# Filler products between the projections ahead of the first scores, and a new order of the third attention's slots, in a two-layer cross-attention transformer kernel

## What is computed

```python
# x: (16, 256, 128), ctx: (16, 64, 64), 16 heads everywhere
x = x + attn0(LN(x), ctx)     # causal self attention (8 channels a head) plus cross attention on ctx, one projection
x = x + ffn0(LN(x))           # silu(x w1) * (x w2) -> gelu(. h1) -> gelu(. h2) -> . w3, hidden 512, ternary weights
u = LN(LN(x)) * g + b         # then, inside the second layer's block:
u = u + mha(u, u)             # self attention, 32 channels a head, masked after the softmax, then a gelu FFN of 512
u = LN(u) * g2 + b2
x = x + u + mha(u, ctx)       # cross attention on 64 context rows, then a gelu FFN of 512
x = x + moe(LN(x))            # top-1 routing over 8 experts with 640 places each, hidden 512
```

## Time and profile before

| what | value |
|---|---|
| median of 3 runs | 1377.05 us (1377.03 to 1378.21) |
| the profiled execution's own time | 1379.22 us |
| its span | 1377.5 us |
| PE busy | 1270.9 us, 92% of the span |
| DVE, ACT, POOL busy | 973.8, 850.3, 656.3 us |
| mean granted TensorE clock | 0.975 of full speed |

### The profile page before, as it was taken

How to read it: one execution, slowest core, us unless ns; L and a number is a source line. 1 busy time by engine, 2 the same in 40 slices (tenths; PEclk the granted TensorE clock), 3 DMA queues, 4 the chain that set the end, 5 groups by cost and what they waited for, 6 DMA issues and landing times.

```text
span 1377.5 us, 43219 instructions
## 1 busy us (share of the span) xinstructions
PE 1270.9 (92%) x18030; PEld 826.5 (60%) x18030; DVE 973.8 (71%) x2245; ACT 850.3 (62%) x1333; POOL 656.3 (48%) x1129
## 2 busy tenths in 40 slices
PE   7999999997999999899999999989978888899895
PEld 4455555554455554456777777766755666676584
DVE  6788888875555554577888888766568887687343
ACT  3687777776666665657777777755456666542352
POOL 4456665633000002236667676544536776355265
PEclk6999999998999999999999999999999999999998
DMA  7000000000600000000011011012001111122451
GB/s 231 6 3 4 3 3 3 4 3 2 172 5 1 1 1 1 1 1 18 19 34 33 19 33 33 19 36 75 1 15 50 49 48 48 48 88 89 150 170 42
DMA packets 64097, 53.80 MB, mean 39 GB/s; under 512 B 10023, under 2 KB 58155, under 8 KB 63648
## 3 DMA queue, kind: packets, MB, share of 16 engines
q1 hardware_dynamic: 60000, 44.21, 11.0%
q0 software_dynamic: 2816, 6.11, 1.3%
q10 hardware_dynamic: 1088, 0.72, 0.2%
HBM read 20.35 MB, written 14.49 MB: 25 GB/s over the span
## 4 chain that ended last, share of the span: by engine, by line
PE 75%; DVE 13%; ACT 4%; issue 3%; POOL 3%; DMA 1%; SPq 0%; POOLq 0%; DVEq 0%; ACTq 0%
PE psum L1575 7%; PE psum L1603 4%; DVE a_nm L623 4%; PE psum L1236 4%; PE psum L960 4%; PE psum L962 4%; PE psum L961 4%; PE psum L1198 3%; PE psum L2696 3%; PE psum L381 2%; PE psum L1546 2%; PE psum L2051 2%; PE psum L535 2%; PE psum L1587 2%; PE psum L2671 1%
## 5 line engine op out<-in xcount | busy, mean ns | idle before, releaser
L1658 DVE TENSOR_REDUCE b_nm<-psum 128x4 f16<-128x1024 f32 x128 | 156.6, 1223 | 52.3 <-PE psum L1580 51.6
L740 ACT ACTIVATE a_prob<-psum 128x768 f32<-128x768 f32 (+1 forms) x160 | 136.1, 853 | 50.3 <-PE psum L467 48.6
L623 DVE TENSOR_REDUCE a_nm<-psum 128x4 f16<-128x1024 f32 (+1 forms) x96 | 117.2, 1222 | 26.2 <-PE psum L480 24.9
L792 POOL TENSOR_SCALAR_AFFINE_SELECT a_prob<-a_prob 128x512 f32<-128x512 f32 x128 | 84.4, 660 | 106.2 <-ACT a_prob L740 106.0
L171 POOL TENSOR_TENSOR f_ln_rstd<-f_ln_tmp,pow_half 128x4 f32<-128x4 f32 x24 | 24.4, 1018 | 194.0 <-DVE f_ln_tmp L160 193.9
L1088 ACT ACTIVATE xo_sb<-psum,f_w_h_s 128x512 f32<-128x512 f32 x64 | 44.0, 688 | 88.3 <-PE psum L962 88.3
L1575 PE MATMUL psum<-b_QTh,b_KTh 32*128 32x256 f16 x512 | 70.4, 272 | 7.3 <-DVE b_nm L1658 5.2
L1580 PE MATMUL psum<-b_KTh,b_QTh 32*128 32x256 f16 x512 | 70.7, 273 | 1.2 <-DVE b_nm L1658 1.2
L1580 PE MATMUL psum<-b_KTl,b_QTh 32*128 32x256 f16 x512 | 69.3, 268 | 0.0
L1580 PE MATMUL psum<-b_KTh,b_QTl 32*128 32x256 f16 x512 | 69.3, 268 | 0.0
L1575 PE MATMUL psum<-b_QTh,b_KTl 32*128 32x256 f16 x512 | 69.3, 268 | 0.0
(11 more groups left out here) (470 smaller groups left out, 4490.8 us busy)
## 6 DMA issues: line engine op xcount, KB each, us to landing
f_h_wh<-b_rden SPq DMA_DIRECT2D x64, 128.0 KB, 2.1
f_h_wh<-c_rden SPq DMA_DIRECT2D x128, 64.0 KB, 2.0
expert_in<-empty SPq DMA_DIRECT2D x8, 662.5 KB, 10.1
m_xt<-expert_in SPq DMA_DIRECT2D x7, 662.5 KB, 5.8
m_w<-in_L_ffn_w_dram SPq DMA_DIRECT2D x16, 256.0 KB
x_sb<-in_x_dram SPq DMA_DIRECT2D x8, 256.0 KB, 4.5
f_w_h_w<-in_L_ffn_h_w_dram SPq DMA_DIRECT2D x2, 1024.0 KB, 7.7
out_dram<-m_send SPq DMA_DIRECT2D x8, 256.0 KB, 2.9
```

Source lines behind the costliest of these rows:

```text
L623: nc.vector.tensor_reduce(out, psum[:, banks, :].rearrange("p i (a b) -> p i a b", a=groups), X, ALU.max, negate=True).then_inc(max_done, 1)
L740: nc.scalar.activation(prob[unit % 5][:, :, 0:width], psum[:, first:first + 2, 0:width], ACT.Exp, scale=SCALE).then_inc(exp_done, 1)
L792: nc.gpsimd.affine_select(out=diagonal, in_=diagonal, compare_op=ALU.is_ge, fill=0.0, base=0, pattern=[[0, 4], [1, P]], channel_multiplier ...
L1658: v.tensor_reduce(self.nm[:, :, :].rearrange("p t (j r) -> p j t r", r=32)[:, 2 * e:2 * e + 2, :, g], self.pr.psum[:, 2:4, :].rearrange("p ...
```

## The change

Four edits, none of which changes a result:

1. In `l0_attention`, each projection or transpose that PE issues in the slots below 0 is followed by one product of constants into bank 4 (nine behind the first `ck`). There are 25 such parts, so 33 products of 512 columns.
2. In `l0_ffn`, DVE's part of the second attention's slot -26 (the normalisation `b_zi` of batch 0) is issued behind the low half of the last gated product instead of ahead of it.
3. In `SelfAttention`, batch 0's `z` goes from slot -18 to -19 and its `q0` and `k0` from slot -16 to -15 (with their ACT copies and, one slot on, their low halves on DVE).
4. In `CrossAttention`, `nm` goes from slot -2 to -3, where the table puts it ahead of `o`; batch 0's `nm` goes to slot -1, behind the next batch's `k`, `q0` and `q1`. The statistics of the context and of the second norm (parts 2 and 3) go from slot -18 to -19, that is ahead of the low half of `k` and of `c_zi`. ACT's copy of `nm` moves with it, ahead of the copy of `o`.

```diff
--- before.py
+++ after.py
@@ -561,6 +561,8 @@
             tensor_values(n - 1, G)
         for use in projections(n, u):
             tensor_projection(use)
+            if n < 0:
+                tensor_warm(pr, 4, 9 if use == ("ck", 0) else 1)
         for m, batch in last_maxima(n, u):
             tensor_max(batch, m)
 
@@ -901,7 +903,7 @@
     LAST = SLOTS - 2
     CLOSE, LAST_CLOSE = (3, 3, 7, 7, 8), (1, 1, 1, 1, 1)
     PRO = spread(1, 0.7, 1.0, SLOTS)
-    NORM = (10, 13)
+    NORM, AFTER_LOW = (10, 13), (NB - 2, 7)
     after.tokens_done, after.sums_free, after.done = added, y_out, LAST
 
     def next_slot(n, slot):
@@ -1051,6 +1053,8 @@
                             vector_low_first(n, slot // 2 - 1)
                     if slot == 8:
                         vector_low_first(n, 3)
+                    if (n, slot - 1) == AFTER_LOW:
+                        after.vector_slot(next_slot(n, slot - 1))
                     if n == NB - 1 and slot == SLOTS - 1:
                         after.vector_slot(next_slot(n, slot))
                     if slot >= 8:
@@ -1066,7 +1070,7 @@
                 if 2 <= n + 2 < NB:
                     for k in at(NORM, slot):
                         early.vector_normed(n + 2, k)
-                if next_slot(n, slot) is not None and (n, slot) != (NB - 1, SLOTS - 1):
+                if next_slot(n, slot) is not None and (n, slot) not in ((NB - 1, SLOTS - 1), AFTER_LOW):
                     after.vector_slot(next_slot(n, slot))
 
 
@@ -1393,7 +1397,7 @@
     VALUES = {0: 3, 1: 5, 2: 7, 3: 9}
     VECTOR = {"rden": 13, "scaled": 16, "output": 23, 0: -28, 1: -26, 2: -22, 3: -20}
     EARLY = {"o": 15, "rden": 9, "scaled": 12, "biased": 13, "output": 16}
-    SOONER = 19
+    SOONER, FIRST_SLOT = 19, {"z": -19, "q0": -15, "k0": -15}
     FIRST_MAX, FIRST, LAST = -9, -28, 8 * (B - 1) + 16
 
 
@@ -1457,9 +1461,10 @@
         early = [(part, n) for part in slots if part in self.EARLY for n in (B - 2, B - 1) if s == self.U * n + self.EARLY[part]]
         if "o" in slots and s == self.U * (B - 3) + self.SOONER:
             early.append(("o", B - 3))
+        early += [(part, 0) for part in slots if part in self.FIRST_SLOT and s == self.FIRST_SLOT[part]]
         return [(part, batch) for part, batch, rest in pairs
                 if rest == 0 and 0 <= batch < B and (batch < B - 2 or part not in self.EARLY)
-                and (part, batch) != ("o", B - 3)] + early
+                and (batch or part not in self.FIRST_SLOT) and (part, batch) != ("o", B - 3)] + early
 
     def bank_of(self, use):
         return self.pr.psum[:, (5, 7)[self.ring.slot(use)], :]
@@ -1863,12 +1868,12 @@
 
 
     U, G, D = 8, 4, 32
-    SLOT = {"v": -7, "z": -13, "o": 21, "nm": -2, "k": -10, "q0": -9, "q1": -9}
+    SLOT = {"v": -7, "z": -13, "nm": -3, "o": 21, "k": -10, "q0": -9, "q1": -9}
     COPIED = {**SLOT, "v": -6}
     SCORES, VALUES, MAXIMA, FIRST_MAXIMA = {0: 0, 1: 1}, {0: 2, 1: 4}, -5, -4
     BANKS = (4, 5)
-    OUTPUT, SCALED, LAST_SLOT = 22, 12, {"o": 14, "scaled": 11, "output": 16}
-    NORMED, RSTD = {0: -33, 1: -26, 2: -18, 3: -18, 4: -15}, -32
+    OUTPUT, SCALED, LAST_SLOT, FIRST_SLOT = 22, 12, {"o": 14, "scaled": 11, "output": 16}, {"nm": -1}
+    NORMED, RSTD = {0: -33, 1: -26, 2: -19, 3: -19, 4: -15}, -32
     FIRST, LAST = -29, 8 * (B - 1) + 16
 
     tail, steps, tail_vector, tail_gpsimd = 8 * B - 2, 8 * B - 1, 8 * B - 11, 8 * B - 9
@@ -1930,8 +1935,10 @@
         last = self.U * (B - 1)
         pairs = [(part, *divmod(s - slot, self.U)) for part, slot in slots.items()]
         return [(part, batch) for part, batch, rest in pairs
-                if rest == 0 and 0 <= batch < B and (batch < B - 1 or part not in self.LAST_SLOT)] + [
-            (part, B - 1) for part in slots if part in self.LAST_SLOT and s == last + self.LAST_SLOT[part]]
+                if rest == 0 and 0 <= batch < B and (batch < B - 1 or part not in self.LAST_SLOT)
+                and (batch or part not in self.FIRST_SLOT)] + [
+            (part, B - 1) for part in slots if part in self.LAST_SLOT and s == last + self.LAST_SLOT[part]] + [
+            (part, 0) for part in slots if part in self.FIRST_SLOT and s == self.FIRST_SLOT[part]]
 
     def bank_of(self, use):
         return self.pr.psum[:, (6, 7)[self.ring.slot(use)], :]
```

## The result

The changed kernel takes 1371.95 us (median of 7 runs, 1368.74 to 1374.64), the kernel before beside it 1379.83 (7 runs, 1377.03 to 1383.75). The ratio is 0.9943, interval 0.9924 to 0.9962: 7.9 us faster. Forecast were 1358 us and a gain of 18.9. The direction was right and the size was not, and the range (1353.5 to 1368) missed. The profiled execution took 1373.46 us, 5.8 less than the profiled one of before.

A forecast was written before the change was run, and what follows sets the result against it. PE, busy 92% of the span, was taken as the bound, so gains come from its waits and half clock. 2.7 + 4.3 + 3.3 + 8.6 = 18.9 us off 1379.22 gave 1360.3, median 1358; range 1353.5 to 1368.

The forecast's parts named there:

- Third attention: CrossAttention loop: early statistics and `nm` ahead of `o` shorten the period from 11.15 to 10.40 us; 8.6 us gained.
- So the period is 10.40 by both ways: Third attention: an observed period and a summed loop both give 10.40 us, so the two edits don't add up.
- The second way: Third attention: an observed 10.40 us period before, with no batch left for `c_zi`, shows what early statistics are worth.
- The first way: Third attention: summing the loop closed by POOL, from copy of `o` through deviations, `z`, `nm` and `o`, gives 10.4 us.
- Rival 2: Third attention bound elsewhere: only the wait before `k` goes, 4.2 us; 1362.5 us in all, chance 0.15.
- the value 0 for batch 0's `nm`: Third attention's start: PE's 3.52 us wait for the first maxima is not shortened; value 0, between -1 and +1.
- The opening: Before the first scores: fillers hold the full clock, worth 5.5 us less 2.8 for relapses; 2.7 us gained.
- two relapses: Opening: two falls of the clock, each as long as that from 38.4 to 41.8 us, costing 1.4 us each.
- No later stage takes it back: Whole kernel: the summed 18.9 us gain survives, PE being busy behind the merges and routing starting when its tokens come.
- Rival 1: Opening at the lower clock throughout: fillers cost 5 us instead of bringing 2.7; 1366 us in all, chance 0.2.
- The merges: First FFN, groups 6 and 7: `b_zi` behind the low half gains 4.3 us, batch 0's `z`, `q0`, `k0` moves 3.3.
- Rival 3: Third attention: `nm` ahead of `o` makes PE wait for the maxima; slower, 1381 us, chance 0.05.

The follow-up runs named there:

- stat_only: The changed kernel with `nm` behind `o` again in the third attention, batch 0 as the others, statistics still early; 1382.41 us, ratio 0.9957 to the kernel before.
- scaled_late: The changed kernel with DVE's multiplication for `c_oT` moved behind the reciprocal and the early statistics; 1386.08 us, ratio 0.9974 to the kernel before.
- scaled_mid: The changed kernel with DVE's order maxima, early statistics, multiplication for `c_oT`, reciprocal in the third attention; 1375.43 us, ratio 0.9885 to the kernel before.
- after_again: The changed kernel, unchanged, run and profiled a second time; 1383.17 us, ratio 0.9938 to the kernel before.
- no_fill: The changed kernel without its filler products in the opening; 1383.74 us, ratio 0.9952 to the kernel before.
- third_old: The changed kernel with the third attention's order and statistics as before; 1383.77 us, ratio 0.9959 to the kernel before.
- mid_oldnm: scaled_mid with `nm` behind `o` again in the third attention, batch 0 as the others; 1378.75 us, ratio 0.9893 to the kernel before.
- mid_nine: scaled_mid with only the nine fillers behind the first `ck`, without the 24 single ones; 1365.07 us, ratio 0.9886 to the kernel before.
- low_first: The kernel before with only DVE's attention step (`b_zi`) moved behind the low half in the FFN's last group but one; 1384.75 us, ratio 0.996.
- before_again: The kernel before, unchanged, run and profiled a second time; 1390.26 us, ratio 0.9994 to the kernel before.
- fill_only: The kernel before with the filler products alone; 1390.97 us, ratio 0.9996 to the kernel before.

## Why the prediction was wrong, step by step

**Third attention: 8.6 forecast.** The step that failed is "So the period is 10.40 by both ways". The second way was a period of before in which `c_zi` had no batch left. I read from it that POOL didn't wait, and not that DVE had 1.1 us less to do there; its multiplication took 2.08 us in just that batch (at 1169.20), unnoticed because DVE had room:

```profile
1169.20 2.08 DVE L2199 TENSOR_TENSOR f_h_wl<-f_h_wh 128x1024 f32<-128x1024 f32 x1
```

```profile
1169.15 0.42 POOL L2284 TENSOR_TENSOR c_cTl<-c_cTw,c_cTh 64x128 f16<-64x128 f32 x1 [3.70 <-ACT c_zTh L2227]
```

The first way summed POOL's and PE's loop and gave DVE no sum of its own. That sum (10.95 less 0.60 of waiting) is 10.35 us busy with 0.87 of it lost beside POOL; it closes the loop. Shown by stat_only (10.95 without `nm`), scaled_late (the loss moved to POOL, 11.07) and scaled_mid (0.1 of the loss left, 10.43). scaled_mid also takes the statistics ahead of the multiplication, but so does scaled_late, and in the profile after POOL did not wait for them, so their place is not what gave the 0.5. From the first score product of batch 0 to that of batch 15 the profiles take 161.4 to 164.1 us with the old loop (five, mean 163.0), 160.1 to 163.4 with the new one (three, 162.3), and 156.3 to 159.6 with the multiplication moved (six, 157.4). So 5.6 of it came when the multiplication had its place. Two smaller things are in the shortfall. `nm` ahead of `o` lengthens the last distance by 0.7 us and more (7.61 before, 8.50 after), which the sum had at nothing. And in the profile after the first three distances took 35.4 us with the DMA wait and the fall of the clock, against 32.3 in after_again.

Rival 2 had this outcome (the loop bound elsewhere) at 0.15 and priced it at 4.2 us. The offset over this stage changes by -1.1, -4.2 and -0.2 us in after, after_again and no_fill, and by -0.5 to +1.2 in the profiles with the old loop; the means are 2.4 apart, and third_old's ratio says 2.9. So 1 to 3 is borne out, and the price was too kind.

The Trainium skill, "SBUF — State Buffer" (SBUF: two separate sides), says that DVE and GpSimd share one pair of ports as an exclusive lock, held for the whole instruction, also by a DVE instruction with two inputs in SBUF against a GpSimd one that reads SBUF, and that the loser stands. SBUF is the memory in which the tiles of these rows lie. This case's rows agree: 1.21 against 2.08 us for this multiplication, 0.42 against 1.19 for POOL's difference, by which started first.

Within that term, `nm` ahead of `o` was to spare the 0.4 us wait before `k`. It does (the wait is gone), but by mid_oldnm's distance of 10.40 the wait had cost nothing in the loop with the multiplication moved. And the value 0 for batch 0's `nm` fits, the wait ahead of the first scores being 3.6 instead of 3.5 us.

**The opening: 2.7 forecast, some 1.3 found and not settled.** The step that failed is the base of the sum: 5.5 us if the clock held, less two relapses before the first scores, with nothing behind them. In the profile after the clock stayed full from 9 to near 26 us, and one fall came before the scores instead of two. By the offsets it was 2.3 us ahead over 26 to 33 us, where the sum had 1.9 + 1.6 = 3.5, 1.1 ahead behind that fall, and 1.65 at the first scores. Then the fall at 46 us took 2.4 (the offset is +0.7 over 46 to 60 us), the one at 63 us 1.1 (+1.8), and the one at 305 us 1.3 (+3.1). They came in each of the nine profiles with the single fillers bar scaled_mid, which lacks the one at 63. "No later stage takes it back" was wrong for this term.

The first scores at 42.47, from which the gain was counted, were also the latest of six profiles without fillers. What the sum had as 2.7 there is 0.6 by the means (41.0 without, 40.4 with). Why the falls come where they do is open. That fillers in the opening cause the later ones is not shown, since three of the six profiles without fillers fall near 45 us too, and two of these near 65 and 307 as well.

Rival 1 (half clock throughout) stayed out, though four of the five parts behind the second `qk` are transposes; the prediction counted three. With the nine products alone (mid_nine) the clock fell at 15 us already, so in these profiles the single ones did hold it.

**The merges: 4.3 + 3.3 forecast.** Right in the sum, with their new waits and the clock, against the same profile: 7.45. The split is not shown. low_first, the first merge alone, got 5.56 of it, which leaves 1.9 for the second, and no run has the second alone. And the falls of the clock in these groups differ between the profiles of the old code, as said of before_again: against it and fill_only the same code gains 5.2 and 6.1, and third_old against fill_only, by ratios and across series, 5.1. So 5 to 7.5 is what runs get, and that 7.6 met 7.45 so closely is in part luck.

The sum by these: 5 to 7.5 for the merges, 1 to 3 for the third attention and 0 to 2 for the opening, which is 6 to 12.5; 7.9 was measured. Rival 3 (slower) stayed out: PE waits 0.5 us for the maxima, not 1.8.

## What to carry to other kernels

When a change takes a wait out of a loop, sum each engine's busy time over one period, not only the chain that closes it now; the engine with the least slack is the next bound, and a period that is short for another reason proves nothing about it. Where DVE and GpSimd both work out of SBUF, an edit that shifts one of them by a few tenths of a microsecond can turn round which of them stands: look at the durations of long two-input DVE instructions in both profiles, and put them where GpSimd is idle. Terms that rest on the clock in a single profile want a second profile of the same kernel first.

## What the runs showed that I had not expected

- The granted clock's course differs between executions of one program, and with it the time: in 26 runs of the kernel before on one chip the mean clock went from 0.963 to 0.980 and the time from 1394.4 to 1387 us, nearly in step.
- Half clock over 24 us of the opening, PE busy 85% of them, cost only 0.2 to 0.6 us at the first scores (40.96) against profiles without fillers that had it for 10 to 17 us (40.34 to 40.72). Over 26 to 33 us it was 1.6 to 1.9 us behind those; it made up the rest behind 34 us, at the full clock, while each of them had another fall at 36 us. So first scores alone don't show what the clock is worth in the stretch ahead of them.
- The multiplication stood past both of POOL's differences: it ends at 1100.50, the second of them at 1099.42, and its own work is 1.2 us. It did not get in between the two.
